# Logits of one head as a 32-row tile of the PE array, in place of block-diagonal keys

## The reference, cut to what matters

```python
qp = einsum('bld,ed->ble', layernorm(x), Wq)          # 1024 tokens, d = 128, 16 heads of 8
idx = argmax(einsum('bld,bmd->blm', qp, kv), axis=-1) # over 6404 memory rows
mem = kv[idx]                                         # one row for each token
mk, mv = split(einsum('bld,ed->ble', mem, Wkv), 2)    # one key and value of 8 for all heads
attn = softmax(einsum('bhld,bmd->bhlm', qh, mk) / sqrt(8), axis=-1)
x = x + tanh(g_xattn) * (einsum('bhlm,bmd->bhld', attn, mv) @ Wc.T)
x = x + tanh(g_ffn) * moe(layernorm(x))               # router of 3 layers, top 2 of 8 experts
```

## Time and profile before

| | |
|---|---|
| median of 3 runs | 364.11 us (363.5 to 366.73) |
| span of the profiled execution, first to last instruction | 361.7 us |
| PE, DVE, ACT, POOL busy | 296.7, 225.2, 160.0, 73.7 us |
| mean granted clock of TensorE | 0.920 |

### The profile page before, as it was taken

How to read it: one execution, slowest core, us unless ns; L and a number is a source line. 1 busy time by engine, 2 the same in 40 slices (tenths; PEclk the granted TensorE clock), 3 DMA queues, 4 the chain that set the end, 5 groups by cost and what they waited for, 6 DMA issues and landing times.

```text
span 361.7 us, 5234 instructions
## 1 busy us (share of the span) xinstructions
PE 296.7 (82%) x1771; PEld 220.4 (61%) x1771; DVE 225.2 (62%) x701; ACT 160.0 (44%) x332; POOL 73.7 (20%) x156
## 2 busy tenths in 40 slices
PE   0397999999998424778999999998888993899994
PEld 0276888988887213646666665554336442488993
DVE  4848778889888778797778877120120106985444
ACT  1155544554455202464766666876215110116540
POOL 3970044445554504000000000000042200000000
PEclk9999999999999655598999999999999896599999
DMA  8992000000000000000000000000000000000002
GB/s 260 384 338 68 3 16 16 15 15 2 15 15 17 15 0 23 1 2 4 4 3 2 4 3 5 0 2 0 0 6 1 2 0 0 1 2 0 2 1 60
DMA packets 9770, 11.78 MB, mean 33 GB/s; under 512 B 1048, under 2 KB 6746, under 8 KB 9738
## 3 DMA queue, kind: packets, MB, share of 16 engines
q1 hardware_dynamic: 8852, 9.98, 8.4%
q0 software_dynamic: 480, 1.25, 1.2%
q10 hardware_dynamic: 406, 0.16, 0.2%
HBM read 10.73 MB, written 0.52 MB: 31 GB/s over the span
## 4 chain that ended last, share of the span: by engine, by line
PE 69%; DVE 16%; issue 6%; ACT 4%; DMA 3%; POOL 1%; DVEq 0%; POOLq 0%; ACTq 0%
PE ps L1246 7%; PE ps L1349 7%; PE ps L1293 7%; PE ps L1211 6%; PE ps L1213 6%; PE ps L1212 6%; PE ps L1325 5%; PE ps L1432 3%; PE ps L1456 3%; PE ps L1450 2%; PE ps L1477 2%; PE ps L1241 2%; PE ps L1398 2%; DVE xn L755 2%; DVE kv_nat L944 2%
## 5 line engine op out<-in xcount | busy, mean ns | idle before, releaser
L691 ACT ACTIVATE kv_nat<-ps 128x512 f32<-128x512 f32 x96 | 52.2, 596 | 26.3 <-PE ps L1349 26.0
L1211 PE MATMUL ps<-shared,q_hi 128*128 128x400 f32 (+1 forms) x128 | 47.5, 371 | 6.4 <-DVE best L814 5.4
L610 ACT ACTIVATE gain<-ps 128x400 f32<-128x400 f32 (+1 forms) x64 | 32.3, 506 | 34.8 <-PE ps L1213 34.6
L814 DVE CUSTOM_DVE_ANT_0 kv_nat<-ps,gain 128x400 f32<-128x400 f32 (+1 forms) x64 | 35.0, 569 | 15.2 <-ACT gain L610 9.8
L1213 PE MATMUL ps<-shared,q_lo 128*128 128x400 f32 (+1 forms) x128 | 44.3, 346 | 0.0
L1212 PE MATMUL ps<-shared,q_hi 128*128 128x400 f32 (+1 forms) x128 | 44.1, 345 | 0.0
L956 DVE TENSOR_REDUCE mx<-ps 128x2 f32<-128x768 f32 x42 | 38.9, 954 | 7.7 <-PE ps L1325 6.9
L1349 PE MATMUL ps<-q_rows,k_blk 128*128 128x256 f32 x192 | 35.5, 301 | 0.0
L1349 PEld LDWEIGHTS ps<-q_rows,k_blk 128*128 128x128 f32 x192 | 29.1, 194 | 5.5 <-ACT kv_nat L691 4.6
L1211 PEld LDWEIGHTS ps<-shared,q_hi 128*128 128x128 f32 x128 | 24.0, 188 | 12.5 <-DVE best L814 10.8
L1293 PE MATMUL ps<-kv_nat,v_ext 128*32 128x256 f32 x384 | 30.7, 391 | 0.2 <-ACT kv_nat L691 0.2
(11 more groups left out here) (276 smaller groups left out, 531.7 us busy)
## 6 DMA issues: line engine op xcount, KB each, us to landing
kv_nat<-in_ctx_dram SPq DMA_DIRECT2D x5, 640.0 KB, 8.0
ew_sb<-in_L_ffn_eW_dram SPq DMA_DIRECT2D x1, 2048.0 KB, 12.6
rw_sb<-in_L_ffn_rW_dram SPq DMA_DIRECT2D x1, 1024.0 KB, 8.2
x_sb<-in_x_dram SPq DMA_DIRECT2D x1, 512.0 KB, 4.4
out_dram<-fin SPq DMA_DIRECT2D x4, 128.0 KB, 1.9
rw_sb<-in_L_ffn_rW_dram SPq DMA_DIRECT2D x1, 256.0 KB, 5.9
pair<-in_ctx_dram,at POOLq DMA_INDIRECT x8, 2.8
q_rows<-shared SPq DMA_DIRECT2D x8, 16.0 KB
```

What stands on the lines that cost most here:

```text
L610: act.activation(gain[:, m % 3, 0:end - start], ps[:, b:b + end - start], ACT.Relu).then_inc(s_rl, 1)
L691: act.activation(probs[:, u % 2, b * HB:(b + 1) * HB, :], bank(4 + n % 2), ACT.Exp, scale=SCALE).then_inc(s_ex, 1)
L814: dve.tensor_tensor_reduce(out=m_all[b2][:, start:end], in0=ps[:, b:b + end - start], in1=gain[:, m % 3, 0:end - start], scale=1.0, scalar ...
L1211: pe.matmul(o, q_h, hi, start=True, stop=False)
```

## The change

`k_blk` and `kd_blk` become `k_rows` and `kd_rows`, dense, with all four copies of a key in one column of 128 partitions. They need no zeros, so the two memsets of GpSimd go, and each key tile is written by one VectorE instruction over 128 partitions in place of four over 32. One head is picked by reading 32 partitions of both operands, `q_rows[r]` and `k_rows[r]`, so a product is a 32-row tile of the array. Each head writes a PSUM bank of its own. Logits now go to banks 2 and 3 or 4 and 5, and the Exp reads 256 columns of each of two banks. In the opening a head's score and gain lie beside each other in one bank; ScalarE starts when both heads are there. In the main stage the jobs have one place, banks 0 and 1, where they had two places of two banks; VectorE reduces each head by itself (384 elements, two instructions a job) and frees its bank by itself; TensorE waits for the first bank ahead of the first matmul and for the second ahead of the second (`bank_free`). Some buffers of the early stage get their own memory.

```diff
-        kd_blk = sba("kd_blk", [P, GH, HALF], F32R)
+        kd_rows = sba("kd_rows", [P, HALF], F32R)
...
-        k_blk = sba("k_blk", [P, GH, TOK], F32R)
...
+        k_rows = sba("k_rows", [P, TOK], F32R)
...
         def place_of(T, m):
 
-            return m % (4 if m in jobs_at(T, -1) else 2)
+            return m % 4 if m in jobs_at(T, -1) else 0
+
+        def banks_of(T, m):
+
+            return 2 if T <= 4 and max_jobs(T)[m][1] is not None else 1
+
+        def banks_used(T, m):
+
+            return sum(banks_of(T, k) for k in range(m))
...
-            pool.memset(kd_blk[:].bitcast(F32), 0.0)
...
-                    if t == 2:
-                        pool.memset(k_blk[:].bitcast(F32)[:, :, 0:T * P], 0.0).then_inc(s_kz, 1)
...
-                        act.wait_ge(s_p1d, rises_before(T, m) + 1)
-                        w = (2 if T <= 4 else 1) * T * P // 2
-                        b = (2 * place_of(T, m) + 1) * HALF
-                        act.activation(rise[:, place_of(T, m), 0:w], ps[:, b:b + w], ACT.Relu).then_inc(s_p1r, 1)
+                        act.wait_ge(s_p1, banks_used(T, m) + banks_of(T, m))
+                        hk = T * P // 2
+                        if T <= 4:
+                            d = bank(2 * place_of(T, m), 2).rearrange("p (h k) -> p h k", h=2)[:, :, hk:2 * hk]
+                            act.activation(rise[:, place_of(T, m), 0:2 * hk].rearrange("p (h k) -> p h k", h=2), d,
+                                           ACT.Relu).then_inc(s_p1r, 1)
...
                                 act.wait_ge(s_lg, n + 1)
-                                act.activation(probs[:, u % 2, b * HB:(b + 1) * HB, :], bank(4 + n % 2), ACT.Exp,
+                                lg = bank(2 + 2 * (n % 2), 2).rearrange("p (h l) -> p h l", h=2)[:, :, 0:W]
+                                act.activation(probs[:, u % 2, b * HB:(b + 1) * HB, :], lg, ACT.Exp,
                                                scale=SCALE).then_inc(s_ex, 1)
...
-                dve.wait_ge(s_kz, 1)
...
-                    for j in range(GH):
-                        r = slice(RS * j, RS * (j + 1))
-                        dve.scalar_tensor_tensor(out=k_blk[r, j, c], in0=ps[r, b:b + P], scalar=k_low[r, 0:1],
-                                                 in1=k_a[r, t % 2, :].bitcast(F32), op0=ALU.mult, op1=ALU.add)
+                    dve.scalar_tensor_tensor(out=k_rows[:, c], in0=ps[:, b:b + P], scalar=k_low[:, 0:1],
+                                             in1=k_a[:, t % 2, :].bitcast(F32), op0=ALU.mult, op1=ALU.add)
...
-                for j in range(GH):
-                    r = slice(RS * j, RS * (j + 1))
-                    last = dve.scalar_tensor_tensor(out=kd_blk[r, j, 0:hk], in0=ps[r, 0:hk], scalar=k_low[r, 0:1],
-                                                    in1=kd_a[r, 0:hk].bitcast(F32), op0=ALU.mult, op1=ALU.add)
-                last.then_inc(s_kdb, 1)
+                dve.scalar_tensor_tensor(out=kd_rows[:, 0:hk], in0=ps[:, 0:hk], scalar=k_low[:, 0:1],
+                                         in1=kd_a[:, 0:hk].bitcast(F32), op0=ALU.mult, op1=ALU.add).then_inc(s_kdb, 1)
...
-                    dve.wait_ge(s_p1, m + 1)
+                    done, place = banks_used(T, m), place_of(T, m)
                     if unit is not None and by_rise(T, m):
+                        dve.wait_ge(s_p1, done + banks_of(T, m))
                         dve.wait_ge(s_p1r, rises_before(T, m) + 1)
...
+                            b, k = (2 * place + j - j0) * HALF, slice((j - j0) * hk, (j - j0 + 1) * hk)
+                            dve.tensor_tensor_reduce(out=rise[:, place, k], in0=ps[:, b:b + hk],
+                                                     in1=rise[:, place, k], scale=1.0, scalar=LOWEST,
+                                                     op0=ALU.add, op1=ALU.max,
+                                                     accum_out=mx[:, i, NG * j + g:NG * j + g + 1]).then_inc(s_p1u, 1)
...
+                        for j in range(j0, j1):
+                            dve.wait_ge(s_p1, done + j - j0 + 1)
+                            b = (2 * place + j - j0) * HALF
+                            dve.tensor_reduce(mx[:, i, NG * j + g:NG * j + g + 1], ps[:, b:b + T * P], AX.X, ALU.max
+                                              ).then_inc(s_p1u, 1)
...
+                opening = len(jobs_at(T, -1))
+
+                def bank_free(m, second):
+
                     if m < opening:
                         if m >= 4:
-                            pe.wait_ge(s_p1u, m - 3)
-                    else:
-                        pe.wait_ge(s_p1u, max(opening, m - 1))
+                            pe.wait_ge(s_p1u, banks_used(T, m - 3))
+                        return
+                    if m == opening:
+                        pe.wait_ge(s_p1u, banks_used(T, opening))
+                        return
+                    before = m - 1
+                    while second and before > opening and banks_of(T, before) == 1:
+                        before -= 1
+                    both = second or T > 4
+                    pe.wait_ge(s_p1u, banks_used(T, before) + (banks_of(T, before) if both else 1))
+
+                def max_job(m):
+
+                    i, unit = jobs[m]
+                    b = 2 * place_of(T, m)
+                    bank_free(m, False)
...
                     g, j0, j1 = heads_of(T, unit)
-                    if by_rise(T, m):
-
-                        for b, keys, done in ((2 * place_of(T, m) + 1, kd_blk, s_p1d), (2 * place_of(T, m), k_blk, s_p1)):
-                            o = ps[:, b * HALF:b * HALF + hu * hk].rearrange("p (j k) -> p j k", j=hu)
-                            pe.matmul(o, q_rows[:, g, i * P:(i + 1) * P], keys[:, j0:j1, 0:hk], start=True, stop=True
-                                      ).then_inc(done, 1)
-                        return
                     for j in range(j0, j1):
+                        r, own = slice(RS * j, RS * (j + 1)), (b + j - j0) * HALF
+                        if j > j0:
+                            bank_free(m, True)
+                        tokens = q_rows[r, g, i * P:(i + 1) * P]
+                        if by_rise(T, m):
+                            gains = own + (hk if T <= 4 else HALF)
+                            pe.matmul(ps[:, gains:gains + hk], tokens, kd_rows[r, 0:hk], start=True, stop=True)
+                            pe.matmul(ps[:, own:own + hk], tokens, k_rows[r, 0:hk], start=True, stop=True
...
-                            b = 2 * place_of(T, m) + j - j0 + c // HALF
-                            last = pe.matmul(ps[:, b * HALF:b * HALF + w], q_rows[:, g, i * P:(i + 1) * P],
-                                             k_blk[:, j, c:c + w], start=True, stop=True)
-                    last.then_inc(s_p1, 1)
+                            last = pe.matmul(ps[:, own + c:own + c + w], tokens, k_rows[r, c:c + w],
+                                             start=True, stop=True)
+                        last.then_inc(s_p1, 1)
...
-                                    col = (4 + n % 2) * HALF + (j - b * HB) * W
-                                    last = pe.matmul(ps[:, col:col + W], k_blk[:, j, t * P:(t + 1) * P],
-                                                     q_rows[:, g, q * W:(q + 1) * W], start=True, stop=True)
+                                    r, col = slice(RS * j, RS * (j + 1)), (2 + 2 * (n % 2) + j - b * HB) * HALF
+                                    last = pe.matmul(ps[:, col:col + W], k_rows[r, t * P:(t + 1) * P],
+                                                     q_rows[r, g, q * W:(q + 1) * W], start=True, stop=True)
                                 last.then_inc(s_lg, 1)
```

More of the change, by code:

```diff
@@ L127, in program @@
         wk_rep = sba("wk_rep", [P, GH, RS])
-        kd_blk = sba("kd_blk", [P, GH, HALF], F32R)
+        kd_rows = sba("kd_rows", [P, HALF], F32R)
         q_rows = sba("q_rows", [P, NG, TOK], F32R)
[L130 to L135, removed]
-        k_blk = sba("k_blk", [P, GH, TOK], F32R)
+        gain = sba("gain", [P, 3, CHUNK])
+        q_nat = sba("q_nat", [P, NT, D])
+        q_a = sba("q_a", [P, HALF], F32R)
+        pick_p = sba("pick_p", [P, NT, P], BF16)
+        q_x = sba("q_x", [P, HALF])
+        k_rows = sba("k_rows", [P, TOK], F32R)
         q_hi = sba("q_hi", [P, TOK], F32R)
@@ L340, in max_turns @@
             jobs = max_jobs(T)
-            return [jobs.index((TQ * (q + 1) - 1, None)) + 1 for q in range(NQ)]
+            return [banks_used(T, jobs.index((TQ * (q + 1) - 1, None)) + 1) for q in range(NQ)]
         def jobs_at(T, step):
@@ L348, in upto @@
             def upto(x):
-                return min(n, max_turns(T)[0] + LEAD + -(-(x + 1) * n // steps))
+                return min(n, max_jobs(T).index((TQ - 1, None)) + 1 + LEAD + -(-(x + 1) * n // steps))
             return range(0 if step < 0 else upto(step - 1), upto(step))
@@ L655, in rise_of @@
                     if by_rise(T, m):
```

(41 more changed lines are left out.)

11 lines of the change are left out of this document (2 added, 9 removed).

## The result

The changed kernel takes 396.06 us (median of 4 runs, 394.76 to 398.26), the kernel before 364.9: a ratio of 1.086, interval 1.080 to 1.093. The prediction was 366.5, range 358 to 376.

The account below looks back on a forecast made before the run. TensorE was taken to set the main stage's pace, with DVE slack. Terms -2.7 - 0.4 + 6.5 - 1.0 = +2.4 on a span of 361.7 gave 364.1, plus 2.4 to the median: 366.5 us, range 358 to 376.

Parts of the forecast that it names:

- Key set-up, -2.7: Key set-up: fewer DVE key writes let it end 2.7 us earlier, bounds 2.3 and 3.3.
- Opening, -0.4: Opening: PE's tiled products spare DVE some early waits, 0.4 us gained, bounds 0 and 0.8.
- Main stage, +6.5: Main stage: DVE and PE handovers with one place add 4.0 us, token tiles 2.5; bounds -1.6 and +12.5.
- logits at 0.47: Main stage: variant with a logits group as slow as before, 0.47 us, giving a cycle of 3.99 us.
- the chain: Main stage: token tiles' DVE work and waits now hold the next refill; +2.5 us charged, bounds 0 and 5.
- logits group of 0.25: Main stage: four tiled logits products assumed to take 0.25 us against 0.47, within a cycle of 3.77 us.
- The clock, a rival at 0.13: Main stage: waits in each job lower the granted clock for over half the cycles, +11 us, total 377.5; chance 0.13.
- a granted clock below 0.95 in the stage: Main stage: a sign listed as showing the prediction wrong, a granted clock under 0.95.
- The cycle at the low clock: Main stage: in the clock rival, weigh and refill nearly double and a cycle takes about 5.2 us.
- No overlap: Rival: tiles don't run side by side, main-stage cycle 3.99 us, total 371.0 us; chance 0.16.
- Tail, -1.0: Tail: shorter logits groups remove part of ACT's waits, 1.0 us gained.
- theory rows: Expectation tested by b2 and b3, not in the prediction: the clock depends on how much of the array is in use.

Follow-up runs that it names:

- e1: The changed kernel with every product over 128 rows, block-diagonal keys and the key set-up of the kernel before: 378.16 us, ratio 1.038 to the kernel before.
- e5: e1 with only the four logits products of a step as 32-row tiles: 389.74 us, ratio 1.060 to the kernel before.
- e9: The kernel before with one place of two banks for main-stage jobs instead of two, joint reduction, 128-row products: 388.08 us, ratio 1.061.
- e2: The kernel before with main-stage job products reading 32 rows of queries and block-diagonal keys instead of 128: 369.80 us, ratio 1.013.
- b2: The kernel before with dense keys and opening tiles only, plus 20 products over 32 rows, one row group, between opening and main stage: 367.82 us.
- b3: As b2, but 80 products over 32 rows, in turn through four row groups and four banks: 367.14 us.
- e6: e1 with only the jobs, in opening and main stage, as 32-row tiles: 391.82 us, ratio 1.071 to the kernel before.
- e3: The changed kernel with three additional 128-row products ahead of the weigh in two of three steps: 430.62 us, no ratio.

## Why the prediction was wrong

- **Bounds of the kernel before: right.** The main stage was TensorE's, with DVE's slack behind two places.
- **Key set-up, -2.7: right,** measured -3.2.
- **Opening, -0.4: a small miss, and the wrong way.** From the first product to the end of the last L944 (L948 in the changed kernel) it took 0.9 us longer. The clock never rose in it, and DVE waited 3.0 us for ACT where it had waited 1.8.
- **Main stage, +6.5: the failed step.** It measured +30.0, in two terms. The handover was worked out well and priced too low: for logits at 0.47 the working gave a cycle of 3.99, and e1, which is that case, showed 4.10. That is 16 x 0.58 = 9.3 us; what is left of the 13.1 is 3.8, where 2.5 was charged for the chain. The forecast's logits group of 0.25 was only a small part of the fault: tiles measured 0.32 at full clock, and e5's cycle, with 128-row jobs, 3.94 where the forecast had 3.77. The other 16.9 had no term in the sum at all: every part of the stage was priced at full clock.
- **The clock, a rival at 0.13, was the larger term.** The prediction named its sign, a granted clock below 0.95 in the stage, and it came: 0.50. The rival was right in kind, but waits were only a part of its cause. e1 has the waits (DVE 11.4 us, cycle 4.10) and holds 1.0; e9 has more of them and holds 0.98. What both lack is the tiles. e2 has tiled jobs without new waits and holds 1.00 as well. The cycle at the low clock was put at 5.2 and measured 5.27; but I let it hold for half of the cycles, and it held for all. Had b2's question been asked of the trace, no row would have answered it: the products of the kernel before span 128 rows, but for six single ones of 0.2 to 0.3 us.
- **"No overlap": wrong.** Four tiles overlap fully in b3, and take 0.32 for 0.47 in e5. A cycle near the 3.99 of this rival came all the same, in e1, with 128-row products.
- **Tail, -1.0: right for full clock** (e5 24.0 against e1's 24.9), wrong here: half of it ran at 1.2 GHz, 28.5 against 25.3 in the kernel before.
- The rest of the span, which the change doesn't touch, came out 2 to 3 us longer, and the set-up started 1.1 later; neither was followed up.

**Still open:** what share of tiles and pauses the clock bears, and whether a main stage of tiles alone with two places would hold it. e2, e5 and e6 lie between hold and fall, and in the changed kernel's tail the clock rose with logits in tiles and fewer pauses. e3's 128-row products should by theory rows have helped more than they did; I can't say why they didn't, so theory rows isn't the whole rule. The 16.9 us put to tiles are a difference of two kernels that also differ in overlap; since that helps the tiles, the low clock alone costs more than 16.9.

## What to carry to other kernels

Cutting a product to 32 rows lets four run side by side in the array, but the gain comes only if four are at hand at once. Tiles with waits between them left the clock at half in the whole stage here, and then all other products pay; tiled jobs among full-height products without waits (e2) left it up. So read the granted clock by stage after such a change, not the busy share. Put such tiles where another engine sets the pace anyway (the opening here), and keep full-height products where TensorE does. And count buffers before instructions: in an in-order queue a second place was worth 23.5 us where splitting the reduction cost nothing.

## What the runs showed that I had not expected

- 6.8 us of gapless 32-row products, recorded as 100% busy, leave the granted clock at 0.50; the same columns over 128 rows, or four times as many products over four row groups in turn, bring it to 1.00 before the burst ends or as it ends.
- 80 tile products of 384 columns take 6.26 us, 0.078 each, at half clock for most of it; 20 in one row group take 6.76.
- 128-row logits behind a 32-row job take 0.67 us instead of 0.47.
- TensorE busy for 80% of a stretch at clock 0.98 (e9), and for 92% at 0.50 (changed kernel).
